# Edge tiles cut at fixed multiples of 128, with the tile that two node blocks share gathered once and copied by ScalarE

## What is computed

```
xp    = layernorm(x) @ W                      # 4 heads of 64
alpha = leaky_relu(a_src[src] + a_dst[dst])   # per edge and head, self loops included
w     = softmax of alpha over the edges of one target
x1    = x + elu(segment_sum(xp[src] * w, dst) + bias)
wt    = layernorm(x1) @ wr + br               # one weight per node
out   = x1n + (wt if among the best 6249 else 0) * (gelu(x1n @ w1 + b1) @ w2 + b2)
        # x1n = layernorm(x1); out also adds x1
```

## Time and profile before

| | us |
|---|---|
| runs, median of 3 | 3182.54 (3172.71 to 3183.56) |
| profiled execution | 3182.05 |
| its span in the trace | 3180.3 |
| PE busy (share of span) | 2095.3 (66%) |
| PEld busy | 1777.2 (56%) |
| DVE busy | 1597.0 (50%) |
| POOL busy | 1596.4 (50%) |
| ACT busy | 722.8 (23%) |
| mean granted TensorE clock | 0.789 of full |

### The profile page before, as it was taken

How to read it: one execution, slowest core, us unless ns; L and a number is a source line. 1 busy time by engine, 2 the same in 40 slices (tenths; PEclk the granted TensorE clock), 3 DMA queues, 4 the chain that set the end, 5 groups by cost and what they waited for, 6 DMA issues and landing times.

```text
span 3180.3 us, 39382 instructions
## 1 busy us (share of the span) xinstructions
PE 2095.3 (66%) x10886; PEld 1777.2 (56%) x10887; DVE 1597.0 (50%) x3933; ACT 722.8 (23%) x1899; POOL 1596.4 (50%) x1675
## 2 busy tenths in 40 slices
PE   8646766657666666676676666766657567676675
PEld 6535655546556555565555555655556555565564
DVE  7654545444454454544544545445445454454556
ACT  5301221212212222122121221221212212122123
POOL 3465545455454554545545545455455454554530
PEclk9867878777787787777877878778778787787788
DMA  7643333333333333333333333333333333333329
GB/s 244 189 123 106 106 104 105 102 105 107 102 106 104 105 104 104 105 103 108 103 103 102 110 99 106 104 105 101 105 103 105 106 102 102 99 109 101 107 72 318
DMA packets 216050, 365.42 MB, mean 115 GB/s; under 512 B 62102, under 2 KB 151346, under 8 KB 216019
## 3 DMA queue, kind: packets, MB, share of 16 engines
q0 software_dynamic: 77488, 214.85, 25.7%
q1 hardware_dynamic: 124434, 136.80, 14.0%
q10 hardware_dynamic: 14096, 13.41, 1.2%
HBM read 326.04 MB, written 38.89 MB: 115 GB/s over the span
## 4 chain that ended last, share of the span: by engine, by line
PE 62%; issue 33%; DVE 3%; DMA 0%; ACT 0%; DVEq 0%; ACTq 0%; SPq 0%
PE ag_ps L939 28%; PE h_ps L909 15%; PE y_ps L922 10%; PE lk_ps L890 3%; PE tr_ps L898 2%; PE ag_ps L831 2%; PE ag_ps L952 1%; DVE base L1442 1%; DVE st_b L1056 0%; PE y_ps L924 0%; DMA node_rows<-base 0%; DVE rows L1250 0%; PE tr_ps L854 0%; PE xl_ps L854 0%; DVE rows L1046 0%
## 5 line engine op out<-in xcount | busy, mean ns | idle before, releaser
L637 POOL DMA_INDIRECT rows<-node_rows,ends x1613 | 1555.6, 964 | 1393.8 <-PE ag_ps L939 908.7
L909 PE MATMUL h_ps<-xnT,w1s 128*128 128x128 f32 x3136 | 488.5, 286 | 818.1 <-issue 818.0
L939 PE MATMUL ag_ps<-rows,oh 128*128 128x260 f32 x3322 | 946.2, 454 | 31.2 <-issue 23.2
L909 PEld LDWEIGHTS h_ps<-xnT,w1s 128*128 128x128 f32 x3136 | 421.5, 199 | 820.1 <-issue 808.7
L939 PEld LDWEIGHTS ag_ps<-rows,oh 128*128 128x128 f32 x3322 | 759.0, 232 | 180.9 <-issue 33.6
L1300 DVE SCALAR_TENSOR_TENSOR base<-steps_of_rows 128x256 f32 (+1 forms) x98 | 42.0, 429 | 1365.8 <-ACT steps_of_rows L790 1365.8
L1250 DVE TENSOR_TENSOR rows<-rows,xl_ps 128x768 f32<-128x768 f32 (+2 forms) x685 | 495.6, 793 | 29.1 <-ACT xl_ps L750 18.1
L721 ACT COPY xnT<-tr_ps 128x256 f32<-128x256 f32 x98 | 36.7, 374 | 1428.9 <-PE tr_ps L898 1337.3
L922 PE MATMUL y_ps<-w2s,hT 128*128 128x256 f32 x1568 | 355.4, 379 | 1.6 <-ACT hT L731 1.6
L922 PEld LDWEIGHTS y_ps<-w2s,hT 128*128 128x128 f32 x1568 | 297.4, 190 | 42.5 <-issue 1.8
L1212 DVE TENSOR_TENSOR oh<-xl_ps,dloc 128x2176 f32<-128x2176 f32 x98 | 236.9, 2418 | 0.0
(11 more groups left out here) (206 smaller groups left out, 1380.0 us busy)
## 6 DMA issues: line engine op xcount, KB each, us to landing
dbc<-dst SPq DMA_DIRECT2D x97, 544.0 KB
rows<-node_rows,ends POOLq DMA_INDIRECT x1613
selfr<-node_rows SPq DMA_DIRECT2D x98, 130.0 KB
base<-in_x SPq DMA_DIRECT2D x14, 896.0 KB, 5.8
base<-in_x SPq DMA_DIRECT2D x49, 256.0 KB
ffn_rows<-yb ACTq DMA_DIRECT2D x96, 128.0 KB, 1.7
node_rows<-base SPq DMA_DIRECT2D x13, 910.0 KB, 5.8
out<-base SPq DMA_DIRECT2D x3, 1024.0 KB, 9.2
```

Source lines behind the costliest of these rows:

```text
L637: pool.indirect_dma_start(out=rows[:, b, t, :], out_offset=None, in_=table, in_offset=bass.IndirectOffsetOnAxis(ap=ends[:, b, t, 0:1], axi ...
L909: last = nc.tensor.matmul(h_ps[:, m * P:(m + 1) * P], w1s[:, c, m * P:(m + 1) * P], xnT[:, c, :], start=(c == 0), stop=(c == DC - 1))
L939: product = nc.tensor.matmul(ag_ps[b][:, 0:ROW], oh[:, b, t, :], rows[:, b, t, :], start=(t == 0), stop=False)
```

## The change

The edge list gets padding in front and its tiles of 128 are cut at fixed multiples of 128 for all windows. A window then touches mostly 17 such tiles, at times 16 or 18, and the first and last belong in part to its neighbours. PE, DVE and the buffers get 18 places (`TILES` 18). The window's last tile always stands in place 17 and the earlier ones before it. The tile which a window shares with the window before is the last one there; ACT copies its gathered rows into places 0 and 1 of the other buffer (`carry`). POOL gathers places 2 to 17, and place 1 where the window touches 18 tiles (16 windows of the present input). In place 0 a shifted base (`base0_id`) leaves edges out where they would count twice. Window 0 has both places gathered and window 1 place 1. Counted out: 97 x 16 + 11 in the last window + 16 + 3 = 1582 gathers.

With it change: `ends` comes in one transfer of 144 bytes per partition from a transposed list instead of two; the first window's `ends` and `dbc` are loaded after the table of windows (it must be known where it starts); a few more small VectorE instructions make the table of windows; the sizes of the rooms for the last phase; and there the loads of the rooms that come free last stand ahead of the first store of the output.

```diff
 def sizes(n, e):
     nw = -(-n // P)
-    tiles = -(-e // n) + 1
+    tiles = -(-e // n) + 2
...
-    for size in (1, 2, 2, 3, 3, 3, 3, 3, 3, 3):
+    for size in (2, 2, 2, 3, 3, 3, 3, 3, 3, 3):
...
             def load_ends(w, i, b, first):
                 if known(w, 2):
-                    wait_apart(sp, (gath[b], 16 * (TILES - 1) * i), (gath_last[b], 16 * i), (loc_ok, w - 1))
-                before = tiles_of(w) - 1
-                sp.dma_start(ends[:, b, 0:before, :], edges[bass.ds(first, before * P), :].rearrange("(p t) v -> p t v", t=before)).then_inc(ld_ends[b], 16)
-                with nc.allow_non_contiguous_dma("an edge to a partition"):
-                    sp.dma_start(ends[:, b, before:before + 1, :], edges[bass.ds(first + before * P, P), :].rearrange("(p t) v -> p t v", t=1)).then_inc(ld_ends[b], 16)
+                    wait_apart(sp, (gath[b], 16 * (TILES - 2) * i), (gath_last[b], 16 * (i + 1 - b)), (loc_ok, w - 1))
+                sp.dma_start(ends[:, b, 0:tiles_of(w), :], edges[:, bass.ds(first, tiles_of(w)), :]).then_inc(ld_ends[b], 16)
...
             sp.wait_ge(win_ld, 16)
+            first = first_edge(0)
+            load_ends(0, 0, 0, first)
+            sp.wait_ge(d16_st, 16)
+            load_targets(0, 0, first)
...
+            sp.wait_ge(y_ok, NW)
+            load_free("ffn")
             for c, (first, count, _) in enumerate(ends_with):
                 sp.wait_ge(out_ok, c + 1)
                 sp.wait_ge(blended, pe_done[c])
                 sp.dma_start(nodes(out, first, count), base[:, first:first + count, :]).then_inc(out_st, 16)
-                if c == 0:
-                    sp.wait_ge(y_ok, NW)
-                    load_free("ffn")
...
-                last = tiles_of(w) - 1
-                for t in range(last):
-                    if known(w, 2) and t % FREED == 0:
-                        wait_apart(pool, *([(ld_ends[b], 32 * (i + 1))] if t == 0 else []), (freed[t // FREED], w - 1))
+                for t in range(2, tiles_of(w)):
+                    if known(w, 2) and (t == 2 or t % FREED == 0):
+                        wait_apart(pool, *([(ld_ends[b], 16 * (i + 1))] if t == 2 else []), (freed[t // FREED], w - 1))
                     gather(t, gath[b])
+                if known(w, 1):
+                    wait_apart(pool, (carry_ok, w))
                 if known(w, 2):
                     some = entry(pool, w, 5, 1)
                     with pool.If(some > 0):
-                        gather(last, gath_last[b])
+                        gather(1, gath_last[b])
...
+            def carry(w, i, b):
+                act.wait_ge(gath[b], 16 * (TILES - 2) * (i + 1))
+                if known(w, 1):
+                    act.wait_ge(freed[0], w)
+                nc.scalar.copy(rows[:, 1 - b, 0:2, :], rows[:, b, TILES - 1:TILES, :].broadcast_to([P, 2, ROW])).then_inc(carry_ok, 1)
+
+            def exponentials(w, i, b):
+                if not isinstance(w, int) or w < NW - 1:
+                    carry(w, i, b)
                 act.wait_ge(diff_ok, w + 1)
...
-                before = tiles_of(w) - 1
-                by_tile = oht[:, b, 0:before * P].rearrange("p (e t) -> p t e", t=before)
-                for t in range(before + 1):
-                    last = nc.tensor.matmul(lk_ps[:, VK * t:VK * (t + 1)], by_tile[:, t, :] if t < before else oht[:, b, before * P:(before + 1) * P], node_parts(w), start=True, stop=True)
+                for t in range(tiles_of(w)):
+                    last = nc.tensor.matmul(lk_ps[:, VK * t:VK * (t + 1)], oht[:, b, t * P:(t + 1) * P], node_parts(w), start=True, stop=True)
...
-                nc.vector.tensor_scalar(dloc[:, 0:n], ends[:, b, 0:n, 1], base_id[:, bass.ds(w, 1)], None, ALU.subtract).then_inc(loc_ok, 1)
+                nc.vector.tensor_scalar(dloc[:, 0:1], ends[:, b, 0:1, 1], base0_id[:, bass.ds(w, 1)], None, ALU.subtract)
+                nc.vector.tensor_scalar(dloc[:, 1:n], ends[:, b, 1:n, 1], base_id[:, bass.ds(w, 1)], None, ALU.subtract).then_inc(loc_ok, 1)
```

More of the change, by code:

```diff
@@ L64, in build @@
     FREED = 6
-    COLS = 6
-    MAIN = (TILES - 1) * P
-    LAST = -(-E * (N - (NW - 1) * P) // (N * P)) + 1
+    COLS = 7
+    FAR = 2.0 ** 20
+    LAST = -(-E * (N - (NW - 1) * P) // (N * P)) + 2
+    NCH = EP // P
     CONSTS = 3 + DIGITS
@@ L386, in in_edges @@
         def in_edges(at):
-            return nc.s_assert_within(at, 0, EP - P, skip_runtime_bounds_check_because="a window's tiles begin before its last edge")
+            return nc.s_assert_within(at, 0, NCH - 1, skip_runtime_bounds_check_because="a window's tiles end with that of its last edge")
         def if_exact(eng, body):
@@ L654, in window @@
                 else:
-                    gather(last, gath_last[b])
+                    gather(1, gath_last[b])
+                if isinstance(w, int) and w == 0:
+                    gather(0, gath_last[b])
                 if isinstance(w, int) and w == 0:
@@ L777, in window @@
                     return
-                exponentials(w + 1, 1 - b)
+                exponentials(w + 1, i + b, 1 - b)
                 if known(w, 1):
@@ L797, in _ @@
             nc.scalar.preload_act_table_set(EXP_AND_LN)
-            exponentials(0, 0)
+            exponentials(0, 0, 0)
             two_by_two(act, PAIRS, window, last_peeled=True, first_peeled=3)
@@ L1106, in window_edges @@
+                nc.vector.tensor_copy(wi[0:NW, 6:7], first_f[0:NW, :])
+                then(nc.vector.scalar_tensor_tensor(out=sq[0:NW, :], in0=length[0:NW, :], scalar=float(1 - TILES), in1=fewer[0:NW, :], op0=ALU.add, op1=ALU.add))
+                nc.vector.tensor_copy(wi[0:NW, 0:1], sq[0:NW, :])
                 then(nc.vector.tensor_tensor(length[0:NW, :], length[0:NW, :], first_f[0:NW, :], ALU.subtract))
-                nc.vector.tensor_copy(wi[0:NW, 0:1], first_f[0:NW, :])
-                nc.vector.tensor_scalar(i1[0:NW, 1:2], length[0:NW, :], float(P - 1), None, ALU.add)
+                nc.vector.tensor_scalar(count_f[0:NW, 1:2], length[0:NW, :], 1.0, None, ALU.add)
@@ L1243, in weigh @@
                 dve.wait_ge(ex_ok, w + 1)
+                if not isinstance(w, int) or w < NW - 1:
+                    dve.wait_ge(carry_ok, w + 1)
                 for k, (a, most) in enumerate(PIECES):
@@ L1453 @@
     n, e = arrays["x"].shape[0], arrays["dst"].shape[0]
-    nw, _, ep = sizes(n, e)
+    nw, tiles, ep = sizes(n, e)
+    ahead = P * (tiles - 1)
     arrays["x"] = np.pad(arrays["x"], ((0, nw * P - n), (0, 0)))
-    arrays["dst"] = np.pad(arrays["dst"], (0, ep - e), constant_values=nw * P)
-    arrays["edges"] = np.stack([np.pad(arrays.pop("src"), (0, ep - e)), arrays["dst"]], axis=1)
+    arrays["dst"] = np.pad(np.pad(arrays["dst"], (ahead, 0), constant_values=-1), (0, ep - e - ahead), constant_values=nw * P)
+    arrays["edges"] = np.ascontiguousarray(np.stack([np.pad(arrays.pop("src"), (ahead, ep - e - ahead)), arrays["dst"]], axis=1).reshape(ep // P, P, 2).transpose(1, 0, 2))
     nc = bacc.Bacc("TRN2", target_bir_lowering=False, num_devices=1, dynamic_dma_scratch_size=4096)
```

66 lines of the change are left out of this document (36 added, 30 removed).

## The result

The changed kernel takes 3106.1 us (median of 5 runs, 3104.0 to 3111.5), against 3181.0 of the kernel before (5 runs). The ratio is 0.978, interval 0.976 to 0.980: 2.2% faster.

The account below looks back on a forecast made before the run. Bound: POOL's gathers at 1.25 us each plus 9.67 us per window waiting for PE's sums. Gathers -36, 18th tile +35, start and end +2 gave +1 on 3182.05: 3183 us, range 3147 to 3210.

Parts of the forecast that it names:

- The 18th tile on PE: Added product and lookup per window, partly left over after the gathers land: 0.37 us per window, +35 us (0 to 60).
- Gathers: POOL's bursts in the loop: 32 fewer conditional gathers at 1.12 us each, -36 us.
- The copy: ACT's copy of the shared tile's rows, 0.64 us per window, hidden behind idle time: cost 0.
- Start and end: Later first gather, one more gather and longer DVE work at the start, earlier loads at the end: together +2 us.
- The law of the limp: PE issues a certain number of instructions from the first gather on, then only a trickle until the gathers have landed.
- The third rival: PE's limp starts a fixed 10.9 us after the first gather; extra tile costs +60 to +94 us, 3208; chance 0.2.
- a clock that turns earlier: PE's granted clock: example of a gain from an unseen cause, no size given; chance 0.05.

Follow-up runs that it names:

- e1: Kernel before with only the lookups' layout changed: the 17 lookups read 128 neighbouring columns of oht, not every 16th; 3125.3 us, 0.981 of before.
- e2: Changed kernel with only the lookups' layout undone: the first 17 lookups read with a stride again; 3185.3 us, 1.001 of before.
- e3: Kernel before with only fewer gathers: the 17th gather runs in 16 windows, not 48; 3144.2 us, 0.988 of before.
- e15: Changed kernel plus 16 small matmuls on PE behind product 12 of 18, in a session with the limp; 2936.5 us, 0.915 of before.
- e14: Changed kernel with a pause: POOL's ninth gather of each burst waits until the first eight have landed; with the limp 2784.1 us, 0.867 of before.
- e10: Changed kernel with gathers of a quarter of the bytes from window 2 on, in a session with the limp; 3111.4 us, 0.979 of before.
- e13: The kernel of e8 once more, again in a session without the limp; 2255.2 us, kernel before 2277.0.
- e7: Changed kernel with gathers of a quarter of the bytes from window 2 on, in a session without the limp; 2254.9 us, 0.990 of before.
- e8: Changed kernel with the 18 lookups moved behind the product that releases POOL, in a session without the limp; 2254.3 us, 0.990 of before.

## Why the prediction was wrong

- **The step that failed** is in "The 18th tile on PE": "2 x 0.12 + 1.17 / 17 = 0.31 us". It prices the added lookup at the pace of the old ones and leaves the other 17 at it. In fact sixteen of the 17 lookups change their weights from a stride of 16 columns to neighbouring ones, and the 18 of the changed kernel take 0.74 us in place of 1.23. The stride is 16 x 0.035 us = -0.56 us of lookups in each window. With a clock that turns 1.3 to 1.5 us sooner on the mean after the first of them it comes to -58 us alone (e1) and -74 to -79 in this kernel (e2). I took the edit of `by_tile` for index arithmetic that goes with the new order of edges. "Of what changes its operand's layout, what does it cost?" was not asked.
- By the Trainium skill (SBUF — State Buffer, section Door 1: The DMA port swizzle) a read that goes to a new 16-byte line with each element pays a penalty; 16 bf16 elements are 32 bytes. The trace agrees in direction: a strided weight load of the kernel before lasts 163 ns, its unstrided 17th one 128 (medians). That this is the cause is not shown. The Trainium skill (TensorE: Matmul & The Clock Gate, section Weight-path perf modes) has the fast weight load read its chunks "packed or strided", with no price for the stride; the traces show one, 62 against 27 ns from lookup to lookup.
- **The rest of the sum was right**: without the layout, e2 measured 3185 where I said 3183. Gathers: -36 forecast, -39 measured (e3). The 18th tile: +0.37 per window forecast; between before and e2 windows with 16 gathers grow by 0.37 (29.93 to 30.30), and e2 less e3 is +41 us where I had +37 with the start. Between the last gap of over 0.3 us and the first lookup PE ran 6.1 instructions in such a window, in place of 3.5; I forecast four more, and it was 2.6. The copy: 0.625 us for 0.64, hidden. Start and end: +3.6 and -1.1 for my +2 together.
- **The law of the limp** held as well, as an amount of PE instructions since the first gather: 122 in e15 after 9.2 us, 123 before after 10.7, 125 after the change after 11.2. The third rival (a fixed time) falls with e15. The count is not exact: in e14's unbroken runs it was 109 to 110, after 12.2 us. What I had not seen is that it begins anew after a pause, and that PE's signals come late as well. What the sum drew from the law held; what makes the limp, I didn't know then and the runs don't show.
- **The clock**: I gave 0.05 to "a clock that turns earlier" as a cause unseen. It was part of the gain, but it came with the edit of the lookups (e1, e2) and not by itself.

## What to carry to other kernels

When a diff changes how an operand is read, ask for the group's minimum and median before pricing it: one instruction of the old kernel may have the new form already, as the 17th lookup had (183 against 216 ns). Price each instruction that stands between a landing and a release, also those whose number stays the same. And before tuning to a stall that waits for nothing visible, look at whether it is there in other sessions: here it decides between 3180 and 2277 us, and a cure (two pauses, -16%) costs 18% where the stall is absent.

## What the runs showed of the hardware

- PE issues some 109 to 125 instructions (matmuls and weight loads) from the first of an unbroken run of indirect gathers on, and then one per 0.7 or 1.4 us (368 and 398 of 827 steps in the changed kernel, 1.0 us in the mean) until some 2.4 us after the last gather's end. A pause of 2.4 to 2.7 us in the gathers restores the allowance. It does not depend on the bytes of the gathers (e10), and it is there in some sessions only. The two queues that the trace calls `instruction` moved 31 packets in the changed kernel, none of them between 330 and 2960 us, which speaks against code loading. What causes it stays open.
- With the limp PE's signals come late: 14.2 us after the record's end in the changed kernel (L936), 9.4 in e15 (product 18), 0.01 us without the limp (e13). They rise some 2 us after the end of the last gather of the run.
- Weights in bf16 with a stride of 16 elements: 62 ns from lookup to lookup (24 columns), with neighbouring columns 27, at a granted clock of 0.50.
- The granted clock turned to full 4.2 us after the first lookup with the dense weights and 5.6 us with the strided ones, as means of widely spread values (windows with 16 gathers). With 17 gathers the kernel before and e1 don't differ (5.0 and 4.9).
- One indirect gather of 128 rows takes 0.95 us and 0.30 of issue, with 1040 bytes a row as with 260 (e7: 973 ns mean for 1582 gathers, e8: the same).
